# A four-stage network with Mamba layers: conv taps per block, residual and matrix casts at other half steps

## What is computed

```python
xb, z = split(rmsnorm(x, w) @ in_w.T)            # 512 channels each
xb = silu(conv4(xb) + cb)                        # depthwise, 4 taps in time, causal
delta, Bm, Cm = split(xb @ xp_w.T)               # 16, 16, 16 columns
delta = softplus(delta @ dtw.T + dtb)            # 512 channels
dA = exp(delta[..., None] * -exp(a_log))         # 16 states a channel
mi = delta[..., None] * Bm[:, None, :] * xb[..., None]
v = 0.6 * v + mi ; h = dA * h + v                # for every token
y = (h * Cm).sum(states) + dp * xb
x = x + (y * silu(z)) @ out_w.T
```

## Time and profile before

| what | value |
|---|---|
| time, median of 3 runs | 4737.4 us (4737.3 to 4738.18) |
| the profiled execution | 4734.2 us, of which span 4732.5 us |
| PE busy in the span | 3637.2 us (77%) |
| DVE busy | 2779.8 us (59%) |
| ACT busy | 2001.0 us (42%) |
| POOL busy | 2035.8 us (43%) |
| mean granted clock of PE | 0.868 of full speed |

### The profile page before, as it was taken

One profiled execution on the slowest core, in us unless ns is written; L12 is line 12 of the kernel. 1 busy time (PEld: TensorE's weight loads), 2 busy tenths in 40 slices (PEclk: granted clock), 3 DMA queues, 4 the chain that ended last, 5 costly groups with the idle time before them and its releaser, 6 DMA issues. The chain is left out here.

```text
span 4732.5 us, 95080 instructions
## 1 busy us (share of the span) xinstructions
PE 3637.2 (77%) x29740; PEld 2399.9 (51%) x29741; DVE 2779.8 (59%) x4894; ACT 2001.0 (42%) x4694; POOL 2035.8 (43%) x1225
## 2 busy tenths in 40 slices
PE   6888869838988888888569888888888124888870
PEld 3545546525555555555345555555555123666650
DVE  3444423347777777777557777777776542333324
ACT  2121212136666665656256656565664111323220
POOL 1010100026666666667356767676767223000016
PEclk9878769969999999999779999999999557999995
DMA  1000000111213121312121312121221521000003
GB/s 47 0 0 0 0 20 0 35 44 48 73 48 74 48 74 48 74 48 71 33 64 48 74 48 71 49 72 50 65 57 51 204 87 66 29 29 31 29 30 100
DMA packets 156158, 241.76 MB, mean 51 GB/s; under 512 B 26450, under 2 KB 84082, under 8 KB 153076
## 3 DMA queue, kind: packets, MB, share of 16 engines
q1 hardware_dynamic: 146164, 210.61, 16.4%
q0 software_dynamic: 9600, 26.23, 1.6%
HBM read 118.86 MB, written 36.18 MB: 33 GB/s over the span
## 5 line engine op out<-in xcount | busy, mean ns | idle before, releaser
L893 POOL TENSOR_TENSOR m_hc<-m_h,m_Cb 128x1024 f32<-128x1024 f32 x512 | 1204.9, 2354 | 764.5 <-DVE m_h L1014 446.7
L1014 DVE TENSOR_TENSOR_SCAN m_h<-m_dA,m_hlast,m_bank 128x256 f32<-128x256 f32 x2048 | 1355.0, 727 | 142.8 <-PE m_bank L1295 61.5
L1277 PE MATMUL m_bank<-m_hc,ident 128*128 128x512 f32 x2048 | 1206.0, 678 | 146.3 <-POOL m_hc L893 146.0
L1144 ACT ACTIVATE m_dA<-m_delta,m_rate 128x256 f32<-128x256 f32 x2048 | 894.1, 500 | 15.6 <-DVE m_h L1014 14.7
L1293 PEld LDWEIGHTS m_bank<-m_M,m_U 128*128 128x128 bf16 x8192 | 607.6, 101 | 359.9 <-DVE m_h L1014 220.6
L1293 PE MATMUL m_bank<-m_M,m_U 128*128 128x64 bf16 x8192 | 677.9, 197 | 123.5 <-DVE m_h L1014 112.2
L1295 PEld LDWEIGHTS m_bank<-m_M,m_U 112*128 112x128 bf16 x8192 | 581.2, 101 | 204.8 <-issue 172.8
L1295 PE MATMUL m_bank<-m_M,m_U 112*128 112x64 bf16 x8192 | 678.3, 197 | 0.0
L1277 PEld LDWEIGHTS m_bank<-m_hc,ident 128*128 128x128 f32 x2048 | 338.7, 205 | 195.4 <-POOL m_hc L893 162.8
L1771 POOL DMA_DIRECT2D slots_y<-x_y x72 | 39.0, 541 | 609.8 <-DVE x_y L1870 609.8
L962 DVE SCALAR_TENSOR_TENSOR m_cv<-m_xpre,m_conv,m_cv 128x256 f32<-128x256 f32 x384 | 273.5, 754 | 22.5 <-ACT m_cv L1082 18.0
(11 more groups left out here) (262 smaller groups left out, 5747.6 us busy)
## 6 DMA issues: line engine op xcount, KB each, us to landing
m_Cb<-m_c_rows SPq DMA_DIRECT2D x256, 256.0 KB, 3.2
m_M<-m_Mhi SPq DMA_DIRECT2D x128, 256.0 KB, 4.1
m_M<-m_Mlo SPq DMA_DIRECT2D x64, 256.0 KB, 3.9
m_U<-m_Uhi SPq DMA_DIRECT2D x128, 128.0 KB, 3.2
g_stage<-in_e_w SPq DMA_DIRECT2D x16, 1024.0 KB, 6.9
slots_x<-x_res SPq DMA_DIRECT2D x36, 256.0 KB, 4.2
x_x_in<-slots_x SPq DMA_DIRECT2D x72, 128.0 KB, 2.0
slots_y<-x_y POOLq DMA_DIRECT2D x72, 128.0 KB, 2.0
```

What stands on the lines that cost most here:

```text
L893: nc.gpsimd.tensor_tensor(hc[:, n % 2], h[:, n % RING], Cb[:, g % 2, n % NG, :].unsqueeze(1).broadcast_to([P, KI, CM]), ALU.mult).then_inc ...
L1014: nc.vector.tensor_tensor_scan(h[:, n % RING, m, :], dA[:, n % RING, m, :], VB[(n % 2) * 2 + g][:, (m % 2) * CM:(m % 2 + 1) * CM], hlast[: ...
L1144: nc.scalar.activation(dA[:, n % RING, m, :], delta[:, par, m, :], ACT.Exp, scale=rate[:, m, n:n + 1]).then_inc(s["da_done"], 1)
L1277: last = nc.tensor.matmul(Y[half][:], net.ident[:], hc[:, n % 2, 2 * half:2 * half + 2, :], start=(n == 0), stop=(n == NS - 1))
```

## The change

Three things move, and no instruction is added or taken away but waits. The three taps of the conv on DVE go block by block, in heads 11, 12, 13 and 14, three instructions that depend on each other in each; `conv_done` now counts blocks. The residual goes from tail 9 to tail 11. On ACT near exp goes from head 25 to 24, ln from 26 to 25, the casts to Mhi from 24 and 27 to 26 and 28; on POOL the first Mlo goes from head 25 to 27 and Glo from 27 to 26. Where POOL has two pieces in half steps of one state, Glo now comes ahead of Mlo.

```diff
@@ gpsimd
                     if at == 6:
-                        pool.wait_ge(s["conv_done"], 1 + q * 2)
+                        pool.wait_ge(s["conv_done"], 1 + q * KI)
@@
-                    if at == 25:
+                    if at == 27:
                         matrix_low(q, 0)
-                    if at == 27:
+                    if at == 26:
                         pool.wait_ge(s["ghi_done"], 1 + q + 1)
                         nc.gpsimd.tensor_tensor(Glo[:], Gf[:].rearrange("p j i n -> p j (i n)"), Ghi[:],
@@ vector
-                    if at in (11, 13):
-                        g = (at - 11) // 2
-                        dve.wait_ge(s["pre_done"], 1 + q * 2 + g + 1)
+                    if 11 <= at < 11 + KI:
+                        m = at - 11
+                        dve.wait_ge(s["pre_done"], 1 + q * 2 + m // 2 + 1)
                         for k in range(TAPS - 1):
-                            for m in (2 * g, 2 * g + 1):
-                                i = nc.vector.scalar_tensor_tensor(cv[:, m, :], xpre[:, m, k:k + CM],
-                                                                   conv[:, m, k:k + 1], cv[:, m, :], ALU.mult, ALU.add)
+                            i = nc.vector.scalar_tensor_tensor(cv[:, m, :], xpre[:, m, k:k + CM], conv[:, m, k:k + 1],
+                                                               cv[:, m, :], ALU.mult, ALU.add)
                             if k < TAPS - 2:
                                 after(i)
                         i.then_inc(s["conv_done"], 1)
@@ tail on vector, and the last call
-                    if at == 9:
+                    if at == 11:
                         dve.wait_ge(s["out_psum"], 1 + t + 1)
@@
-                tail(NCM, 1, 9)
+                tail(NCM, 1, 11)
@@ scalar
-                        act.wait_ge(s["conv_done"], 1 + q * 2 + 2)
+                        act.wait_ge(s["conv_done"], 1 + q * KI + KI)
@@
-                    if at == 25:
+                    if at == 24:
                         act.wait_ge(s["clamp_done"], 1 + q * 2 + 2)
                         nc.scalar.activation(u[:], delta[:, par], ACT.Exp).then_inc(s["near_done"], 1)
-                    if at == 26:
+                    if at == 25:
                         act.wait_ge(s["near_done"], 1 + q + 1)
                         nc.scalar.activation(u[:], u[:], ACT.Ln, bias=1.0).then_inc(s["ln_done"], 1)
-                    if at in (24, 27):
-                        j = (at - 24) // 3
+                    if at in (26, 28):
+                        j = (at - 26) // 2
                         act.wait_ge(s["mf_done"], 1 + q * TM + j + 1)
```

## The result

The changed kernel takes 4768.1 us in the median of six runs (4760.1 to 4776.7); the kernel before took 4737.8 beside it. The ratio is 1.0059, with an interval of 1.0045 to 1.0072: slower by 0.6%, 28 us (the medians differ by 30). Forecast were 43 us and 4780, with a range of 4712 to 4820. The profiled execution of the changed kernel took 4763.2 us (before 4734.2), so 29 us are to be found between the two profiles.

A forecast was written before the change was run, and what follows sets the result against it. PE bounds the kernel except at two holes a chunk. Terms +1.9 (hole A), -0.5 (hole B), 0 (residual) gave +1.4 a chunk, +42 over 30 chunks, +1 for prologues: 4777 profiled, 4780 median, range 4712 to 4820.

The forecast's parts named there:

- hole A: PE's first gap in a chunk: waits for DVE's scans behind the second conv group (2.65 us), then POOL's product (1.24).
- PE with two holes: PE sets the pace except at two gaps a chunk, on DVE's scans and POOL's u; only moving these moves the kernel.
- Four blocks, four meetings with POOL: DVE's conv taps stand still during POOL tensor_tensors; four taps a chunk over 1.5 us instead of two.
- Hole A, +1.9: PE's gap at DVE's scans and POOL's product grows by 1.9 us a chunk, bounds +0.5 to +3.0.
- 30 chunks like this one: The one chunk read, multiplied by the 30 chunks whose head runs inside the loop: +42 us.
- Its parts, +1.3 waiting and +0.6 clock: PE waits 1.3 us longer for half step 5's scans; one third of a 1.7 us low-clock stretch comes on top.
- Four waits more, 0.5 us of DVE: DVE's conv waits for itself eight times a chunk instead of four, 0.12 more each: +0.5 us a chunk.
- Logarithm ahead of the casts, -0.5: ACT's ln ends 1.8 us earlier, delta 2.0, but PE's second gap, at u, only 0.5; bounds -2.0 and +0.5.
- The rival of the whole 2.0 us: All of delta's 2.0 us reaches u through a sooner cast: 4734 to 4692 us; chance 0.08.
- Residual, 0: DVE's residual two half steps later fills 6.79 us idle but gains nothing, PE being busy; bounds -2.1 and 0.
- Its rival of 2.1 us a chunk: DVE, not PE, limits around the residual, so its 2.1 us gain counts: 4716 us; chance 0.07.
- Prologues, +1: The two prologues, one a layer outside the loop, add waits only: +1 us.

The follow-up runs named there:

- run with short products: Changed kernel with POOL's products of states 0 and 1 cut to 16 columns: 4629.4 us, to be compared only with the kernel before cut likewise (4652.9 us).
- the run with the matrix behind u: Changed kernel with conv taps back in two groups of six, plus POOL's first low matrix moved behind product u (head 27 to 29): 4728.5 us, ratio 0.9966.
- the conv undone: Changed kernel with conv taps back in two groups of six (heads 11 and 13), casts and residual as changed: 4720.8 us, ratio 0.9963.
- the groups earlier: Changed kernel with conv taps in two groups of six, in half steps 0 and 1 instead of 1 and 3: 4640.0 us, ratio 0.9783.
- control with short products: Kernel before with POOL's products of states 0 and 1 cut to 16 columns: 4652.9 us, ratio 0.9815.

## Why the prediction was right, point by point

The direction and the mechanism came out as forecast, the size at two thirds (28 us for 43). Inside hole A the waiting was taken too large and the clock too small, and these two misses offset each other; that the sum for hole A came so close is in part luck.

- **What bounds the kernel.** PE with two holes: right. Whatever didn't move a hole (the residual, the waits) hardly moved the time, and what moved hole A moved it most.
- **Four blocks, four meetings with POOL.** Right in the chunk read, to 0.1 us: block ends, the scans of half steps 4 and 5 and PE's new wait at 2508.3 came where the working put them. The run with short products shows the cause: block 3 goes from 3.32 to 1.50, and the sign of the change turns with POOL's two instructions.
- **Hole A, +1.9.** In chunks as the one read +2.0, but the mean is +1.59. The step that was too large is "30 chunks like this one": in 10 of 30 PE is behind at this place, block 1 gets through and PE's waits even fall, by 0.34. The kernel before showed which ten, as its gate waited for PE in them.
- **Its parts, +1.3 waiting and +0.6 clock.** The matmuls behind PE's new wait start 1.3 us later, as forecast (2508.31; the working had 2507.0 for before), but in idle time of PE the chunk read has 1.05 more, and the 30 have 0.55 more in the mean. The clock adds the rest, about 1.0 in both. The prediction priced one more low stretch at 1.7 and took a third of it. By the 21 chunks with equal waits about 3.4 us more at the low clock cost 1.0, and in the mean 2.85 us came on top (4.55 to 7.40).
- **Four waits more, 0.5 us of DVE.** They are in the timeline (a block alone takes 1.50), but cost the kernel nothing that can be told. The rule of the Trainium skill (VectorE: DVE Perf Modes, "The DRAIN you can't avoid") by which they cost nothing isn't borne out by DVE's rows (0.51 from start to start, against 0.40 without the wait); the kernel's time can't tell.
- **Logarithm ahead of the casts, -0.5.** -0.6 in the chunk read, -0.78 in the mean. Mechanism as forecast: ln 1.8 earlier, u held by the low matrix, which the run with the matrix behind u confirms. The rival of the whole 2.0 us didn't happen. Whether it would have paid stays open: in that run a sooner u was given back, but there the low matrix came later, which a sooner cast would not bring with it.
- **Residual, 0.** Within 0.2%, by its run perhaps 8 us of gain. Most of it stands in the stretch from the transposes to the in-projection (33.52, against 33.88), where the residual doesn't lie; left open. Its rival of 2.1 us a chunk is out.
- **Prologues, +1.** They took 5 us. PE's waits in the two stretches of both layers grew by 0.2 us in all, as small as forecast. What the term left out is the clock: the time at the low level there rose from 31.8 to 43.7 us. How much of that the change brings can't be told, since kernels with the same waits differ: 6.15 and 7.70 us for the first of these stretches in the two layers of the kernel before.
- **The sum.** +1.4 a chunk against +0.73; 42 + 1 against 22 + 5.

## What to carry to other kernels

Read where an instruction with two SBUF operands on VectorE stands against GpSimd's queue, not only how long it is: the same twelve taps a chunk took 276.4 us with the conv undone, 378.3 in the changed kernel and 225.4 with the groups earlier, nearly all by their place. Blocks spread evenly for smoothness can all come to stand right behind the event that releases the other engine; put them where the other engine is known to wait. A hand-written order repeats with more than one phase (here the two chunks of a loop body), so a term read from one chunk has to be read from a second before it is multiplied. And split a hole's growth into TensorE's waits and its time at the low clock before you price it: here 0.55 and 1.04 us a chunk.

## What was not expected of the hardware

Hole A costs more than its length. In the control with short products PE's waits in hole A's stretch fell by 1.23 us a chunk (4.03 to 2.80), all of it the wait for the product; the stretch fell by 2.58 (23.77 to 21.19), and the time at the low clock in it from 4.6 to 1.7 us. And having started a chain of taps doesn't protect the rest of it: in block 2 of the chunk read u times z began 0.26 us after the first tap, and while this first tap took 0.48 us, the second took 2.45; so it was in all 30 chunks.
